# Sizes of the expert matmuls by rank: steps of eight columns down to 240 instead of 288, 288, 272, 272 and four times 256

## The reference

```python
cap = max(1, int(T * CAP_FACTOR / E))                 # 160
top_p, top_i = lax.top_k(softmax(xt @ gate_w), K)     # K = 2
for k in range(K):
    e = top_i[:, k]
    ...                                               # place of each token in its expert
    keep = pos < cap
    buf = zeros((E, cap, D)).at[e, pos_c].set(xt * keep, mode='drop')
    h = gelu(einsum('ecd,edf->ecf', buf, w1) + b1)
    y = einsum('ecf,efd->ecd', h, w2) + b2
    y = y + einsum('ecr,erd->ecd', gelu(einsum('ecd,edr->ecr', buf, wd)), wu)
    out = out + y[e, pos] * keep * top_p[:, k]
out = out + 0.2 * (gelu(xt @ sw1 + sb1) @ sw2 + sb2 + gelu(xt @ swd) @ swu)
return x + out
```

## Time and profile before

| what | value |
|---|---|
| median of 3 runs | 180.77 us (180.49 to 181.28) |
| profiled execution: span from its first to its last instruction | 179.5 us |
| profiled execution: what lies around the span, by the median of the runs | 1.2 us (180.77 less the span's 179.5) |
| TensorE busy | 174.6 us (97%) |
| VectorE, ScalarE, GpSimd busy | 148.4, 145.8, 97.4 us |
| granted TensorE clock in the span | 1.000 |
| eight expert periods | 55.20 to 165.05 us |

### The profile page before, as it was taken

One profiled execution on the slowest core, in us unless ns is written; L12 is line 12 of the kernel. 1 busy time (PEld: TensorE's weight loads), 2 busy tenths in 40 slices (PEclk: granted clock), 3 DMA queues, 4 the chain that ended last, 5 costly groups with the idle time before them and its releaser, 6 DMA issues.

```text
span 179.5 us, 4056 instructions
## 1 busy us (share of the span) xinstructions
PE 174.6 (97%) x1410; PEld 170.0 (95%) x1410; DVE 148.4 (83%) x332; ACT 145.8 (81%) x323; POOL 97.4 (54%) x110
## 2 busy tenths in 40 slices
PE   5999999999999999999999999999999999999994
PEld 6987789999989999999999999999999999999993
DVE  5678999999876779979789699798899889889822
ACT  3379799706779898997899799899899899898930
POOL 5802368210647662087977858958946455164700
PEclk9999999999999999999999999999999999999999
DMA  4594001669828492696878758579597868776242
GB/s 134 151 346 142 0 2 50 201 194 328 268 52 302 112 316 70 227 252 95 279 237 122 285 171 158 188 257 188 137 318 164 231 222 148 248 218 92 31 71 84
DMA packets 25885, 31.84 MB, mean 177 GB/s; under 512 B 4572, under 2 KB 22392, under 8 KB 25864
## 3 DMA queue, kind: packets, MB, share of 16 engines
q1 hardware_dynamic: 21720, 26.22, 45.5%
q0 software_dynamic: 3904, 5.25, 16.9%
q10 hardware_dynamic: 240, 0.10, 0.2%
HBM read 26.31 MB, written 5.24 MB: 176 GB/s over the span
## 4 chain that ended last, share of the span: by engine, by line
PE 88%; DVE 6%; ACT 3%; issue 1%; another core or an unknown queue 1%; POOL 0%; DVEq 0%; POOLq 0%; ACTq 0%
PE y_ps L1038 13%; PE y_ps L1040 13%; PE y_ps L1039 13%; PE hid_ps L1038 8%; PE hid_ps L1040 8%; PE hid_ps L1039 8%; PE turn_ps L1038 4%; PE turn_ps L1040 4%; PE turn_ps L1039 4%; PE y_ps L1046 2%; DVE w_l L703 2%; PE turn_ps L1207 2%; ACT gelu_f L627 1%; ACT hid_h L628 1%; PE hid_ps L1066 1%; PE turn_ps L1066 1%
## 5 line engine op out<-in xcount | busy, mean ns | idle before, releaser
L733 DVE TENSOR_TENSOR hid_l<-gelu_f,hid_h 128x320 fp32r<-128x320 f32 (+2 forms) x88 | 42.8, 501 | 13.8 <-ACT hid_h L628 13.4
L477 POOL DMA_INDIRECT out_rows<-y_row,slot_tok x23 | 38.2, 1662 | 26.8 <-DVE y_row L929 11.9
L463 POOL DMA_INDIRECT slot_in<-slot_rows,slot_src x23 | 33.0, 1435 | 18.5 <-DVE slot_src L889 8.2
L1038 PE MATMUL y_ps<-w_h,hid_h 128*128 128x256 f32 x128 | 36.4, 284 | 0.3 <-DVE hid_l L733 0.3
L1039 PE MATMUL y_ps<-w_l,hid_h 128*128 128x256 f32 x128 | 36.2, 283 | 0.0
L1040 PE MATMUL y_ps<-w_h,hid_l 128*128 128x256 f32 x128 | 36.2, 283 | 0.0
L1038 PE MATMUL hid_ps<-xs_h,w_h 128*128 128x256 f32 (+2 forms) x96 | 27.9, 291 | 0.0
L627 ACT ACTIVATE gelu_f<-hid_ps,bias_s 128x320 f32<-128x320 f32 x48 | 26.1, 543 | 1.9 <-PE hid_ps L1040 1.3
L1039 PE MATMUL hid_ps<-xs_l,w_h 128*128 128x256 f32 (+2 forms) x96 | 27.5, 287 | 0.0
L1040 PE MATMUL hid_ps<-xs_h,w_l 128*128 128x256 f32 (+2 forms) x96 | 27.5, 287 | 0.0
L710 DVE TENSOR_TENSOR w_l<-w_raw,w_h 128x512 fp32r<-128x512 f32 x40 | 26.6, 701 | 0.0
(11 more groups left out here) (239 smaller groups left out, 446.2 us busy)
## 6 DMA issues: line engine op xcount, KB each, us to landing
w_raw<-in_L_ffn_w SPq DMA_DIRECT2D x16, 1024.0 KB
w_raw<-in_L_ffn_sw SPq DMA_DIRECT2D x3, 1024.0 KB
x_in<-in_x SPq DMA_DIRECT2D x2, 512.0 KB, 3.7
w_raw<-in_L_ffn_sw SPq DMA_DIRECT2D x2, 512.0 KB, 7.1
slot_rows<-token_row SPq DMA_DIRECT2D x2, 512.0 KB, 4.1
wu_raw<-in_L_ffn_wu SPq DMA_DIRECT2D x24, 32.0 KB
out_rows<-base SPq DMA_DIRECT2D x1, 512.0 KB
slot_in<-slot_rows,slot_src POOLq DMA_INDIRECT x23
```

Source lines behind the costliest of these rows:

```text
L463: pool.indirect_dma_start(out=slot_in[par][0:n, s, :], out_offset=None, in_=x_rows, in_offset=bass.IndirectOffsetOnAxis(ap=slot_src[0:n, e ...
L477: pool.indirect_dma_start(out=out, out_offset=bass.IndirectOffsetOnAxis(ap=slot_tok[0:n, e, s:s + 1].bitcast(U32), axis=0), in_=y_row[0:n, ...
L733: dve.tensor_tensor(hid_l[:, j - 1, 0:n], gelu_f[:, j % 3, 0:n], hid_h[:, j - 1, 0:n].bitcast(F32), ALU.subtract).then_inc(hid_split, 1)
L1038: pe.matmul(out_ap, l_h, r_h, start=start, stop=False)
```

## The change

The table of sizes becomes 288, 280, 272, 264, 256, 248, 248, 240. The step is 8 columns instead of 16; a rank's size is smaller by one step for each rank up to the fifth, and the last rank has one step more. GpSimd's two operations on `steps_down` compute this (a minimum and a comparison with the last rank, instead of two comparisons), and VectorE's sum is the same.

```diff
-STEP = P // 8
+STEP = P // 16
-STEPS_AT = (2, 4)
-SIZES = [FEW - STEP * sum(r >= s for s in STEPS_AT) for r in range(E)]
+STEPS = 5
+SIZES = [FEW - STEP * (min(r, STEPS) + (r == E - 1)) for r in range(E)]
@@ rank_experts
-                for i, s in enumerate(STEPS_AT):
-                    ins = pool.tensor_scalar(steps_down[:, i, :], rank_at[:, :], float(s), float(STEP), ALU.is_ge, ALU.mult)
-                ins.then_inc(rank_ready, 1)
+                pool.tensor_scalar(steps_down[:, 0, :], rank_at[:, :], float(STEPS), float(STEP), ALU.min, ALU.mult)
+                pool.tensor_scalar(steps_down[:, 1, :], rank_at[:, :], float(E - 1), float(STEP), ALU.is_equal,
+                                   ALU.mult).then_inc(rank_ready, 1)
@@ value_tokens
-                for i in range(len(STEPS_AT)):
+                for i in range(2):
```

## The result

The changed kernel takes 179.5 us (median of 22 runs, 178.73 to 182.43), where the kernel before takes 180.95 us in the same session (22 runs). The ratio is 0.9909, 95% interval 0.9883 to 0.9935: faster by 0.9%. 0.9909 x 180.77 is 179.1 us, and the median as it stands 179.5; 179.6 was forecast. The profiled execution took 179.35 us, with a span of 177.6 us where before it was 179.5. The median of the kernel before is not the same in all sessions of the experiments (180.8 to 185.2 us), and in some of the traces TensorE waits 1 to 2 us in rank 0, before anything that is compared here; so the lengths of single periods carry most of what follows.

What follows compares the result with a forecast made beforehand. TensorE was taken to bound the experts, paid by the moving column. Terms for ranks 1, 3, 5, 6 and 7, 0.33 + 0.33 + 0.18 + 0.18 + 0.15 = 1.17 us, gave 180.77 - 1.17 = 179.6 us, range 179.1 to 180.5.

Steps and rivals of the forecast that it cites:

- the halving of the difference between two periods: Rank 1: ranks 1 and 2 differ by 0.66 us for 16 columns, so 8 columns give 0.33 us.
- the slope of 0.42 ns a column: Ranks 5 and 6: price per moving column between 256 and 512, giving 54 x 8 x 0.42 = 0.18 us each.
- The narrower weights: Second output tile, ranks 5 to 7: 25 matmuls each, 0.02 us, 0.04 at rank 7; costed at nothing, 0.08 kept for range.
- The cover of 0.54 us: Rank 6: time from the last split's end to the matmul needing it, called far more than the 0.18 used up.
- its own sign of being wrong: Wrong if ranks 1 and 3 don't give a third of a microsecond each, or a new wait stands in ranks 5 or 6.
- the cap: Rank 7: of 0.36 us at most 0.19 can be had, as splits keep ScalarE's pace; 0.15 us taken.
- ScalarE's idle 0.57 us: Head of rank 7's period: what a faster TensorE can take before ScalarE bounds these periods, against 0.18 asked per period.
- The floor: Rival, chance 0.27: weight loads already set the 120.0 ns at 256 columns; ranks 5 to 7 give nothing, 180.2 us.
- the fixed part: Floor rival: weight loads cost 0.9 ns a column, 112 ns for a full load, beside a fixed part.
- Plain fp32's price below 256: Rival, chance 0.03: fp32r matmuls below 256 columns cost as plain fp32, 49 us more, about 229 us.
- The long branch: Rival, chance 0.02: an expert exceeds its rank's size, so all run at 320 columns, 201 us.
- Waits: Rival, chance 0.10: ScalarE's lag grows, ranks 5 to 7 give back 0.51 us and restarts cost more, 180.3 us.

Runs made afterwards that it cites:

- early_ranks: The kernel before with sizes 288, 280, 272, 264 and four times 256 (only ranks 1 and 3 smaller): median 183.1 us, ratio 0.9966.
- late_ranks: The kernel before with only ranks 5 to 7 smaller (248, 248, 240 columns): median 183.34 us, ratio 0.9935.
- act288_before: The kernel before with ScalarE's gelus and VectorE's splits of the experts' hidden tiles on 288 columns instead of 320: 181.59 us, ratio 1.0018.
- fine_sizes: The changed kernel with sizes 280, 272, 272, 264, 256, 248, 240, 240 and the limit lowered from 288 to 280: 178.44 us, ratio 0.9843 to before.

## Why the prediction held, and where it didn't

**TensorE bounds the periods and is paid by the column: right.** Ranks 5 and 6 alone gave 0.31 and 0.32 us, and shorter gelus gave the kernel before nothing in ranks 1 to 6 and 0.06 us in rank 7.

**Rank 1, 0.33 us forecast, 0.42 measured.** The step that failed is the halving of the difference between two periods: of the 6.5 ns between 288 and 272 columns (6.3 by the periods), 4.3 lie in the first eight. In the executions of early_ranks the same rank gave only 0.14, by the slow pace of its output.

**Rank 3, 0.33 forecast, 0.49 measured.** The step that failed is the same, the even rise: 272 to 264 columns is 5.1 ns by the output's runs (4.1 by the hidden layer's) and not 3.2.

**Ranks 5 and 6, 0.18 each forecast, 0.31 and 0.26 measured.** The step that was mis-sized is the slope of 0.42 ns a column. The hidden layer gives 54 x 4.7 ns = 0.25 us; the slope was taken between 256 and 512 columns, and 256 lies high, 1 ns above 260. The upper bound of the prediction, 0.24 us from the line of 272 and 288, was the better value. The narrower weights add 0.06 us each; the prediction had put them at nothing, with 0.02 as the bound, from a row of six matmuls of 96 weight columns which shows hardly more gain than 120 give. In rank 6 some 0.06 us are lost again at the head of its output (0.26 against 0.32 in late_ranks), on the release by line 929. The cover of 0.54 us that the prediction gave rank 6 was read at the last split and doesn't apply to this release; its own sign of being wrong, a new wait in ranks 5 or 6, came true by 0.07 us that the view of waits doesn't list.

**Rank 7, 0.15 forecast, 0.08 measured: the cap was right in kind, its place wrong.** I looked for the wait at VectorE's last split, with 0.15 us of cover, and for a wait on hid_l. The wait is of that size and in that rank alone, but it came at the output's first matmul and on line 929, where there was no cover. The view that would have shown it is the timeline of VectorE ahead of that matmul. TensorE then runs at 120.0 ns up to the second tile, from 157.29 to 160.05, so the late splits stop nobody any more. ScalarE's idle 0.57 us was no cover either, though the prediction leant on it: it lies between two periods, and the chain that binds runs inside one. It shrank to nothing at rank 7's head (the row at 151.61 has no bracket). The 0.19 us after the first matmul of the output, which I took for the price of a restart, are that: without the late release the gap is 0.13 us (act288_before). But the kernel before paid it already, so it was no new cost of the change. What the period gained is 0.05 us from ScalarE's earlier start, which the prediction had as 0.04, and 0.03 from its output (163.13 - 157.10 = 6.03 us against 165.05 - 158.99 = 6.06), by the narrower weights.

**The rivals.** The floor exists, at 111.7 ns and not at 120.0: the even 120.0 was not the loads' alone, since 248 columns run at 115.1 (nor the moving columns' alone, since 120 weight columns bring it to 117.5). The 28 ns for 32 weight columns in the earlier trace rows give 112 ns for 128 and 84 for 96, near the floor of 111.7 and the 88 ns; so the fixed part that I had left in doubt doesn't show in the pace. Plain fp32's price below 256 is refuted by every run with such sizes. The long branch isn't taken. Waits take back some 0.35 us in rank 7 (157.10 - 156.63 less a pace of 0.12) and 0.06 in rank 6, a small version of that rival.

**The size.** The five terms come to 1.56 us and not 1.17; all but rank 7's were too low. By them the time would have been 180.77 - 1.56 = 179.2 us. The median of 179.5 is nearer to the forecast of 179.6 than the terms deserve, and that is luck: the kernel before stood at 180.95 in that session and not at 180.77, and medians that scatter by tenths do the rest.

## What to carry to other kernels

A slope between two far sizes is a poor price for a step of eight columns: measure the pace at the very sizes, since it goes in uneven steps and a round size can be dearer than one a little larger. Before a stage is counted as shorter, list everything that the first instruction of the next stage waits for and read when each was released; a release that ends just the usual 0.25 us before it is a wait that doesn't show yet. Work of a fixed size on other engines (here gelus on 320 columns) costs nothing until the bound engine gets shorter, and then it is the next thing to cut.

## What the runs showed of the hardware that I had not expected

- A stream of fp32r matmuls with a fresh load of 128 weight columns each does not go below 111.6 to 111.7 ns, at 236, 232, 224, 208 and 192 moving columns alike; with 96 weight columns 192 moving columns take 88 ns.
- 256 moving columns take 119.6 to 120.0 ns and 260 take 118.8; 284 take 133.1 (one execution) and 288 take 131.8.
- With 256 moving columns, 120 weight columns bring the pace from 120.0 to 117.5 ns.
- The same instructions have two paces at an unchanged granted clock of 1.00: 127.5 and 133.3 ns for the output with 280 moving columns in different executions, 113.3 and 117.9 ns for the tile with 112 weight columns even in one execution (fine_sizes). What picks one is open.
- From the end of VectorE's operation to the start of the matmul that waits for it is 0.25 us in three kernels and 0.25 to 0.27 in the others. Where the release comes just that late without a listed wait, the matmul and the one after it still lose 0.06 us together.
